# Two of five convolution taps of two sequences as diagonal matmuls on TensorE instead of steps on ScalarE and VectorE

## The reference

```python
proj = jnp.einsum('btd,ed->bte', x, W_in)
gate, val = (proj[..., :D], proj[..., D:])
g = jax.nn.sigmoid(gate)
v = conv(val, conv_w, padding 2 on both sides, each feature by itself) + conv_b   # 5 taps
a = jnp.tanh(a_param)
h = a * h + g * v                      # over the tokens: y is the h of every token
res = x + jnp.einsum('btd,ed->bte', y, W_out)
out = layernorm(res) * ln_w + ln_b
```

## Time and profile before

| | us |
|---|---|
| three runs: median (lowest to highest) | 589.87 (589.71 to 591.79) |
| the profiled execution, its own time | 590.07 |
| its span in the trace | 588.3 |
| TensorE busy, share of the span | 523.9, 89% |
| VectorE busy | 467.8, 80% |
| ScalarE busy | 351.7, 60% |
| GpSimd busy | 247.0, 42% |

### The profile page before, as it was taken

The page is one execution under the profiler, slowest core; times in us unless marked ns, Lnnn a source line. Parts: engine busy times, 40 slices in busy tenths (PEclk is TensorE's granted clock), DMA queues, the critical chain, the costliest instruction groups (busy, mean ns, idle before and its releaser), DMA issues.

```text
span 588.3 us, 7310 instructions
## 1 busy us (share of the span) xinstructions
PE 523.9 (89%) x2154; PEld 389.0 (66%) x2154; DVE 467.8 (80%) x819; ACT 351.7 (60%) x630; POOL 247.0 (42%) x240
## 2 busy tenths in 40 slices
PE   6999896758789999999999999999988999678990
PEld 2465454535477887787878778887867787466770
DVE  3899989996788499979988997998785678756781
ACT  3548369395685574767657576736656665436442
POOL 1034020303013356545745555463444267437674
PEclk9999998969889999999999999999998999969995
DMA  8950202110001022000000000002112082156541
GB/s 283 322 160 2 71 1 71 72 72 2 36 37 72 1 72 72 1 1 1 1 1 0 1 2 1 2 0 72 36 36 73 2 295 94 61 171 186 158 140 41
DMA packets 28103, 39.99 MB, mean 68 GB/s; under 512 B 7421, under 2 KB 19838, under 8 KB 27776
## 3 DMA queue, kind: packets, MB, share of 16 engines
q1 hardware_dynamic: 24656, 31.10, 16.7%
q0 software_dynamic: 3408, 8.43, 4.0%
HBM read 25.70 MB, written 16.83 MB: 72 GB/s over the span
## 4 chain that ended last, share of the span: by engine, by line
PE 63%; DVE 10%; ACT 7%; issue 3%; DMA 1%; POOL 0%; SPq 0%; POOLq 0%; DVEq 0%; ACTq 0%
PE psum L1429 41%; PE psum L1507 6%; PE psum L1356 4%; PE psum L1396 2%; PE psum L1180 2%; PE psum L1477 1%; PE psum L1269 1%; PE psum L1344 1%; PE psum L1250 1%; ACT res L568 1%; PE psum L1286 1%; ACT L742 1%; DVE slots_full L1599 1%; DVE slots_full L1854 1%; PE psum L1364 1%
## 5 line engine op out<-in xcount | busy, mean ns | idle before, releaser
L1429 PE MATMUL psum<-slots_hi,w_hh 128*128 128x512 f32 x576 | 184.8, 402 | 3.4 <-ACT slots_hi L641 3.4
L1429 PEld LDWEIGHTS psum<-slots_hi,w_hh 128*128 128x128 f32 x576 | 106.8, 189 | 29.0 <-issue 5.0
L1034 POOL TENSOR_TENSOR gru<-slots_full,gru 128x512 f32<-128x512 f32 x43 | 66.7, 1551 | 134.1 <-ACT gru L774 133.7
L1429 PE MATMUL psum<-slots_lo,w_hh 128*128 128x512 f32 x288 | 114.9, 399 | 0.0
L1429 PE MATMUL psum<-at,v_ih_pair 128*128 128x512 f32 x288 | 91.6, 399 | 0.0
L1429 PEld LDWEIGHTS psum<-at,v_ih_pair 128*128 128x128 f32 x288 | 54.2, 190 | 13.6 <-DVE at L1820 0.4
L1429 PEld LDWEIGHTS psum<-slots_lo,w_hh 128*128 128x128 f32 x288 | 54.5, 189 | 12.9
L1167 PE MATMUL psum<-early_hi,w_in 128*128 128x512 f32 x128 | 58.1, 613 | 5.3 <-DMA early_hi<-in_xT 5.1
L1827 DVE SCALAR_TENSOR_TENSOR gru<-psum,vec,gru 128x512 f32<-128x512 f32 x48 | 35.8, 747 | 33.2 <-PE psum L1429 23.8
L1854 DVE TENSOR_TENSOR slots_full<-gru 128x512 f32<-128x512 f32 x48 | 53.8, 1121 | 1.7
L774 ACT ACTIVATE gru<-gru,vec 128x512 f32<-128x512 f32 x48 | 34.6, 721 | 31.3 <-DVE gru L1834 30.6
(11 more groups left out here) (253 smaller groups left out, 948.1 us busy)
## 6 DMA issues: line engine op xcount, KB each, us to landing
gathered<-sorted_rows SPq DMA_DIRECT2D x39, 129.0 KB, 2.3
x_scratch<-slots_full SPq DMA_DIRECT2D x8, 512.0 KB, 3.0
x_block<-x_scratch SPq DMA_DIRECT2D x8, 512.0 KB, 4.0
early_hi<-in_xT SPq DMA_DIRECT2D x3, 1024.0 KB, 5.3
x_tm<-in_x SPq DMA_DIRECT2D x4, 512.0 KB, 6.9
slots_full<-expert_plus SPq DMA_DIRECT2D x1, 2048.0 KB, 9.5
sorted_rows<-gru SPq DMA_DIRECT2D x1, 1032.0 KB, 11.5
early_hi<-in_xT SPq DMA_DIRECT2D x2, 512.0 KB, 4.4
```

Source lines behind the costliest of these rows:

```text
L1034: pool.tensor_tensor(DF(u), full[:, c, seq(k, h), blk(j)], X(u), ALU.subtract).then_inc(d_pool, 1)
L1429: last = pe.matmul(psum[:, bank, :], w, d, start=start and i == 0, stop=stop and i == len(pairs) - 1)
```

## The change

For the third and fourth sequence (b = 2 and 3, so four pieces) the first two taps move to TensorE. Its weights for them are four diagonal matrices, `eyes[:, i, c]` = identity times the tap's column of weights, made once by ScalarE. When a piece's value has been copied to `val` and its gate matmuls are issued, TensorE reads `val` back, shifted by i columns, and writes the sum of the two taps over the value in banks 2 and 3: four float32 matmuls of 512 columns for a piece. ScalarE then evicts both banks with the bias into `cvs`; this takes the place of the first tap (L543) and stands behind the gate's sigmoids. VectorE adds three taps instead of four. From piece 5, that is (2, 1), on, a piece's value matmuls wait until that eviction of the piece before has freed the banks (`tap_act`).

```diff
+        PE_TAPS = 2
+        eyes = gru[:, 5, :].rearrange("p (i c n) -> p i c n", i=PE_TAPS, c=C)
+        def first_tap(b):
+            return PE_TAPS - 1 if b > 1 else 0
+        def conv_before(n):
+            return TAPS * n - (PE_TAPS - 1) * max(n - 2 * C, 0)
+        def val_before(n):
+            return J * n + max(n - 2 * C, 0)
...
                 def values(b, c):
...
-                    act.wait_ge(val_ev, J * n + J)
-                    if b > 1:
-                        act.wait_ge(scanned, n - 2 * C + 1)
-                    act.activation(cvs[b % 2][:, c, :], val[:, c, 0:T], ACT.Identity, bias=col(c, V_CB),
-                                   scale=col(c, 0)).then_inc(tap_act, 1)
+                    if b < 2:
+                        act.wait_ge(val_ev, J * n + J)
+                        act.activation(cvs[b % 2][:, c, :], val[:, c, 0:T], ACT.Identity, bias=col(c, V_CB),
+                                       scale=col(c, 0)).then_inc(tap_act, 1)
...
+                    if b > 1:
+                        act.wait_ge(scanned, n - 2 * C + 1)
+                        act.wait_ge(val_mm, val_before(n + 1))
+                        act.activation(cvs[b % 2][:, c, :].rearrange("p (j n) -> p j n", j=J), psum[:, VB:VB + J, :],
+                                       ACT.Identity, bias=col(c, V_CB)).then_inc(tap_act, 1)
...
+                    for i in range(PE_TAPS):
+                        for c in range(C):
+                            act.activation(eyes[:, i, c], ident[:], ACT.Copy, scale=col(c, i)).then_inc(neg_set, 1)
...
                 def project(b, lo=0, hi=C):
...
+                                if n > 2 * C and bank == VB:
+                                    pe.wait_ge(tap_act, n)
...
+                        if b > 1:
+                            pe.wait_ge(neg_set, 1 + PE_TAPS * C)
+                            pe.wait_ge(val_ev, J * n + J)
+                            for j in range(J):
+                                for i in range(PE_TAPS):
+                                    last = pe.matmul(psum[:, VB + j, :], eyes[:, i, c],
+                                                     val[:, c, i + j * BANK:i + (j + 1) * BANK],
+                                                     start=i == 0, stop=i == PE_TAPS - 1)
+                            last.then_inc(val_mm, 1)
...
                 def taps(b, c):
-                    for i in range(TAPS):
+                    for i in range(first_tap(b), TAPS):
                         tap_step(b, c, i)
...
-                tap_step(2, 1, 0)
+                tap_step(2, 1, 1)
                 offsets(1)
-                for i in range(1, TAPS):
+                for i in range(2, TAPS):
                     tap_step(2, 1, i)
```

More of the change, by code:

```diff
@@ L422, in load_fm @@
                     if b > 1:
-                        sp.wait_ge(val_mm, J * C * (b - 1))
+                        sp.wait_ge(val_mm, val_before(C * (b - 1)))
                         sp.wait_ge(gate_mm, J * C * (b - 1))
@@ L430, in load_tm @@
                     if b == B - 1:
-                        sp.wait_ge(val_mm, J * C * B)
+                        sp.wait_ge(val_mm, val_before(C * B))
                         sp.wait_ge(gate_mm, J * C * B)
@@ L534, in values @@
                     if b > 0:
-                        act.wait_ge(conv, TAPS * (n - C + 1))
+                        act.wait_ge(conv, conv_before(n - C + 1))
                     for j in range(J):
-                        act.wait_ge(val_mm, J * n + j + 1)
+                        act.wait_ge(val_mm, val_before(n) + j + 1)
                         act.activation(val[:, c, HALO + j * BANK:HALO + (j + 1) * BANK],
                                        psum[:, VB + j, :], ACT.Copy).then_inc(val_ev, 1)
-                    act.wait_ge(val_ev, J * n + J)
-                    if b > 1:
-                        act.wait_ge(scanned, n - 2 * C + 1)
-                    act.activation(cvs[b % 2][:, c, :], val[:, c, 0:T], ACT.Identity, bias=col(c, V_CB),
-                                   scale=col(c, 0)).then_inc(tap_act, 1)
+                    if b < 2:
+                        act.wait_ge(val_ev, J * n + J)
+                        act.activation(cvs[b % 2][:, c, :], val[:, c, 0:T], ACT.Identity, bias=col(c, V_CB),
+                                       scale=col(c, 0)).then_inc(tap_act, 1)
                     if b > 1:
@@ L1246, in value_input @@
                         pe.wait_ge(val_ev, J * C * B)
+                        pe.wait_ge(tap_act, C * B)
                     if i % B >= 2:
@@ L1596, in tap_step @@
                     dve.wait_ge(tap_act, n + 1)
-                    if i:
-                        dve.wait_ge(conv, TAPS * n + i)
+                    if i > first_tap(b):
+                        dve.wait_ge(conv, conv_before(n) + i - first_tap(b))
                     dve.scalar_tensor_tensor(out=cvs[b % 2][:, c, :], in0=val[:, c, i + 1:i + 1 + T],
@@ L1609, in scan @@
                     dve.wait_ge(gate_ev, J * n + J)
-                    dve.wait_ge(conv, TAPS * (n + 1))
+                    dve.wait_ge(conv, conv_before(n + 1))
                     dve.tensor_tensor(cvs[b % 2][:, c, :], cvs[b % 2][:, c, :], gates[:, b % 2, c, :],
@@ L1759, in _ @@
                 residual(2)
-                tap_step(3, 1, 0)
+                tap_step(3, 1, 1)
                 offsets(3)
-                for i in range(1, TAPS):
+                for i in range(2, TAPS):
                     tap_step(3, 1, i)
```

## The result

| | before | after |
|---|---|---|
| median (lowest to highest), four runs each | 590.11 us (589.71 to 591.79) | 596.71 us (595.92 to 598.65) |
| profiled execution, its span | 590.07, 588.3 | 595.92, 593.9 |
| TensorE, VectorE busy | 523.9, 467.8 | 535.9, 463.1 |

The ratio is 1.0115, with a 95% interval of 1.0088 to 1.0142: the change makes the kernel slower.

A forecast was written before the change was run, and what follows sets the result against it. VectorE paced the changed stage up to about 106 us; TensorE would gain four groups (13.7 us) and short waits, of which 5.6 us remain at output(2)'s end: 590.07 to 595.7, 595.5 for the median; range 592.5 to 598.5.

The forecast's parts named there:

- The price of a group: Four diagonal matmuls on TensorE, priced like project(2)'s float32 matmuls of 512 columns: 0.858 us each, 3.43 us a group.
- First half: Up to the end of residual(1): output(1) starts at 74.5 us and residual(1) ends at 83.7, 5.2 us late.
- the 3.77 us: TensorE's time from the start of value_input(0) to the start of output(1), added to reach 74.5 us.
- The fed length of 9.18 us: Time from output(1)'s start to residual(1)'s end when TensorE feeds it, read from output(0): 9.18 us.
- Second half: From there to the end of output(2): it starts at 109.0 us and ends at 116.0, 5.6 us late.
- the wait for the eviction: TensorE standing until ScalarE has evicted the diagonals' banks: 1.2 us before (2,1), 0.35 before project(3) half 1.
- Window(2): On ScalarE behind the last eviction and a table load: ready near 110.0 us and so hidden.
- The transposes: Transposes(0) before output(2) on TensorE: with the pause gone, 1.91 us at full clock instead of 3.56.
- The rule of the Trainium skill: Rival: transposes don't engage full clock, so transposes(0) stay at 3.56 us; 597.2 us in all, chance 0.12.
- The rival in which VectorE stays the bound: Three VectorE taps of 1.33 us leave the chain, 4.0 us saved, 585.9 us in all; chance 0.05.
- all waits are as before: Behind output(2): waits unchanged and no known slack on the chain, so the 5.6 us delay stays to the end.

The follow-up runs named there:

- four_steps: The changed kernel, but VectorE keeps four tap steps in every piece, adding the second tap once more; ratio to before 1.0118.
- third_only: The kernel before with only the third sequence's two taps moved to TensorE, the fourth as before; ratio to before 1.0084.
- fourth_only: The kernel before with only the fourth sequence's two taps moved to TensorE, the third as before; ratio to before 1.0019.
- half_price: The changed kernel with one diagonal matmul a bank instead of two, the first tap left out in the third and fourth sequence; ratio to before 1.0004.
- one_piece: The kernel before with only piece (3,0)'s two taps moved to TensorE, product in banks 4 and 5; ratio to before 0.9999.
- other_banks: The changed kernel with the diagonal products written to banks 4 and 5; ratio to before 1.0051.
- one_piece_warm: one_piece plus filler matmuls nobody reads in two TensorE pauses; ratio to before 0.9973, in a second series 0.9978.
- before_warm: The kernel before plus filler matmuls nobody reads, seven before transposes(1) and two before first_sums; ratio to before 0.9973.
- changed_again: The changed kernel, unaltered, timed once more in another series; ratio to before 1.0109.

## Why the prediction was right

The direction, the mechanism and nearly every time in it held; against 595.5 us forecast stand 596.71, within 592.5 to 598.5, and 5.85 us between the two profiled executions against 5.6. That the 5.85 come so near is in part luck: the end of output(2) was 6.14 us late (110.41 to 116.55), and some of that was given back in a part of the kernel that the forecast took as unchanged.

- The price of a group, 3.43 us, was exact (67.56 to 71.00). The row of the same shape and type was the right one to go by; mostly-zero weights and operands read one column off cost no more and no less.
- First half: output(1) forecast for 74.5, found at 74.60; residual(1) for 83.7, found at 83.78; VectorE's wait of some 6 us found at 6.12. Two small errors offset each other ahead of output(1): value_input(0) began at 71.00, 0.25 us later than forecast, and the 3.77 us from there were 3.60, since the 3.77 of the kernel before ran to the end of a record and not of its slot. The fed length of 9.18 us, read from output(0), carried over to 83.78 - 74.60 = 9.18. That VectorE's saved steps lie in waits is shown by four_steps, not only read.
- Second half: output(2) forecast for 109.0, found at 109.48, though project(2) had started 0.16 us earlier. The term that was too small is the wait for the eviction. Each step of the round trip was a little longer: the eviction takes 1.11 us and not 1.02, it ends at 60.47 and TensorE goes on at 60.62, and in the second half ScalarE's copies came 0.2 us later than forecast (92.32). So TensorE went on at 97.35 and not at 96.75, behind a pause of 1.01 us that I had put at 0.35. Window(2), forecast for 110.0 "and so hidden", came out at 110.96 and was hidden by nothing to spare: VectorE's short instructions behind it let residual(2) start at 111.51, where TensorE's first pair, 2.00 us behind output(2)'s start as in the first half, came at 111.48.
- The transposes ran at full clock, 1.91 us. The window at 107.7 us shows 1.00 as transposes(0) run. The rule of the Trainium skill that I had kept as a rival ("TensorE: Matmul & The Clock Gate", Part 4) does not hold in this form: the trace disagrees with its sentence that full clock does not engage for a transpose. third_only and fourth_only show both cases with the same instructions, 3.68 us behind a pause of 4.65 us and 1.91 us behind matmuls.
- The saving on VectorE was 4.7 us of busy time and 0 of the time. The rival in which VectorE stays the bound needed cheap groups. half_price shows one point on the way: at 1.72 us a group TensorE still decides the first half, VectorE the start of residual(2), and the loss is gone.
- Behind output(2) I had said that all waits are as before. The waits are, the clock isn't: the same instructions between 125 and 134 us took one microsecond more or less from kernel to kernel. The forecast didn't meet this as an error, since the change fared there as before did (4.28 us to 4.01 for value_input), but in the traces one_piece's gain went there. Between the end of output(2) and the attention's first matmul the change lost 0.3 us more, and got 0.8 back in the rest, whose cause I didn't follow.

## What to carry to other kernels

Moving work from a busy engine to one that looks freer pays only as far as the second engine's pauses on the same path reach: here 2.9 us of 15.5 were free, and two groups of 3.4 us with a round trip through an eviction were put in. Before such a move, ask what stands behind the new work on its engine and which instruction of the relieved engine waits for that; a fixed order turns every microsecond saved there into waiting. When the receiver of a product is another engine, give it a bank of its own if one is free: the waits for the release cost 2.87 us here, nearly half of the loss.

## What the runs showed of the hardware

- The granted clock behind a pause decides about small gains. Value_input, behind TensorE's pause of 7.1 us and the four low parts, took 3.69 us (fourth_only), 4.01 (before), 4.93 (one_piece) and 5.30 (other_banks) with the same instructions and the same pause. It is not a trait of the kernel alone: in two traces of one_piece_warm, both with the filler ahead of it, it took 2.74 and 4.72.
- Matmuls that nobody reads, put into that pause, went with a clock of 1.00 through the transposes behind it in two traces (before_warm, one_piece_warm) and 0.67 in a third (one_piece_warm again). In before_warm the clock fell all the same with the last of the four single matmuls, 0.97 us apart, that followed. The two in the pause before first_sums went with 1.98 us in all three traces; without them it was 3.06 to 3.68 in nine traces and 1.98 in one.
- The kernel before took 587 to 592 us in some series and 609 to 619 in the others. Two series, one of each kind (590.63 and 613.60 us), carry the same chip number, so it isn't shown that the chip makes it. Up to the end of residual(2) the stages have the same length in both kinds (69.86 us in both changed_again and four_steps). In four_steps, of a slower series, and changed_again, of a faster, the attention begins at 170.3 and 170.7 us and the span ends at 616.8 and 594.6; by the windows the engines do the same work up to 470 us, so the difference lies behind that, where the tokens are scattered, gathered and pass the experts. What makes it was not tried.
